# An attention layer without transposes on TensorE: the row of shifts goes transposed through memory, results are scaled untransposed, and the last two heads get seven score banks

## The reference, cut to what matters

```python
x = L0_attn_hidden_states                                   # (4, 2048, 256)
xn = layernorm(x)
# attention
qkv = (xn @ W_qkv).reshape(B, S, 3, 16, 16)                  # q, k, v of (4, 16, 2048, 16)
scores = einsum('bhqd,bhkd->bhqk', q, k) + compute_bias(rel_emb, S, S)
attn = softmax(scores, axis=-1)
out = einsum('bhqk,bhkd->bhqd', attn, v)
out = transpose(out, (0, 2, 1, 3)).reshape(B, S, 256) @ W_out
# feed-forward: two layers with gelu, scaled by the sum of the combine weights of the router
x = x + out + ffn(xn)
```

## Time and profile before

| | |
|---|---|
| median of 3 runs | 3451.89 us (3449.85 to 3497.42) |
| the profiled execution, its own time | 3448.83 us |
| its span in the trace | 3447.1 us |
| PE busy | 3245.1 us (94%) |
| DVE busy | 2769.0 us (80%) |
| ACT busy | 2476.0 us (72%) |
| POOL busy | 1203.8 us (35%) |
| first stage | to about 587 us |
| attention | from 587 to 3376 us, first score matmul at 631 us |
| projection | 3376.7 to 3447 us |

### The profile page before, as it was taken

The page is one execution under the profiler, slowest core; times in us unless marked ns, Lnnn a source line. Parts: engine busy times, 40 slices in busy tenths (PEclk is TensorE's granted clock), DMA queues, the critical chain, the costliest instruction groups (busy, mean ns, idle before and its releaser), DMA issues. The chain is left out here.

```text
span 3447.1 us, 56397 instructions
## 1 busy us (share of the span) xinstructions
PE 3245.1 (94%) x20426; PEld 1573.3 (46%) x20426; DVE 2769.0 (80%) x3046; ACT 2476.0 (72%) x4875; POOL 1203.8 (35%) x1644
## 2 busy tenths in 40 slices
PE   8899997699999999999999999999999999999998
PEld 7788886233333333333333333333333333333337
DVE  5477764588888888888888888888888888888815
ACT  4343443588878887888878888788878887888875
POOL 1112121233433344434444344333443334333430
PEclk9999999799999999999999999999999999999999
DMA  7332323100000000000000000000000000000006
GB/s 183 115 88 74 102 82 101 47 28 28 28 28 28 28 28 28 28 28 28 28 28 28 28 28 28 28 28 28 28 28 28 28 28 28 28 28 28 15 1 199
DMA packets 80480, 156.52 MB, mean 45 GB/s; under 512 B 8088, under 2 KB 48728, under 8 KB 73864
## 3 DMA queue, kind: packets, MB, share of 16 engines
q1 hardware_dynamic: 80200, 152.90, 15.5%
HBM read 101.92 MB, written 56.16 MB: 46 GB/s over the span
## 5 line engine op out<-in xcount | busy, mean ns | idle before, releaser
L905 DVE TENSOR_REDUCE max_half<-ps 128x1 f32<-128x1024 f32 x1984 | 2337.2, 1220 | 337.0 <-PE ps L946 333.6
L832 ACT ACTIVATE prob<-ps 128x512 f32<-128x512 f32 x4096 | 2114.8, 603 | 506.9 <-PE ps L962 506.8
L962 PE MATMUL ps<-q_st,k_st 49*128 49x512 f32 x4096 | 1511.3, 446 | 160.7 <-ACT prob L832 52.5
L946 PE MATMUL ps<-k_st,q_st 48*128 48x512 f32 x3968 | 1569.4, 468 | 0.2 <-DVE max_half L905 0.2
L876 POOL TENSOR_TENSOR prob<-prob,near 128x224 f32<-128x224 f32 (+2 forms) x1408 | 965.1, 691 | 1667.8 <-ACT prob L832 1649.0
L962 PEld LDWEIGHTS ps<-q_st,k_st 49*128 49x128 f32 x4096 | 679.2, 184 | 1334.7 <-ACT prob L832 1142.2
L971 PE MATMUL ps<-prob,vx 128*32 128x512 f32 x4096 | 947.8, 606 | 0.0
L971 PE MATMUL ps<-prob,vr 128*32 128x512 f32 x4096 | 946.1, 604 | 0.0
L946 PEld LDWEIGHTS ps<-k_st,q_st 48*128 48x128 f32 x3968 | 656.3, 184 | 58.7 <-DVE max_half L905 2.5
L608 PE MATMUL ps<-xnt,w_parts 128*128 128x512 f32 x1152 | 276.7, 400 | 16.7 <-DMA k_early<-qk_parts 10.5
L608 PEld LDWEIGHTS ps<-xnt,w_parts 128*128 128x128 f32 x1152 | 218.1, 191 | 70.1 <-DMA k_early<-qk_parts 10.7
(11 more groups left out here) (70 smaller groups left out, 1060.4 us busy)
## 6 DMA issues: line engine op xcount, KB each, us to landing
qk_parts<-parts SPq DMA_DIRECT2D x64, 512.0 KB, 4.6
near<-bias_near SPq DMA_DIRECT2D x64, 352.0 KB, 13.4
q_st<-qk_parts SPq DMA_DIRECT2D x64, 256.0 KB
k_st<-qk_parts SPq DMA_DIRECT2D x64, 256.0 KB
x_sb<-in_L_attn_hidden_states SPq DMA_DIRECT2D x18, 512.0 KB, 6.1
base_rows<-x_sb SPq DMA_DIRECT2D x16, 512.0 KB, 2.9
q_st<-qk_parts SPq DMA_DIRECT2D x64, 128.0 KB
k_st<-qk_parts SPq DMA_DIRECT2D x64, 128.0 KB
```

Of the source, the lines that this page charges most:

```text
L832: nc.scalar.activation(prob[:, kb % PROBS, CH * c:CH * (c + 1)], ps[:, tile_at(kb, c) % RING], ACT.Exp).then_inc(drained, 1)
L905: nc.vector.reduce_max(max_half[:, par % 2, i, half:half + 1], ps[:, MAX_BANK + 2 * half:MAX_BANK + 2 + 2 * half].rearrange("p a n -> p (a ...
L946: mm = nc.tensor.matmul(ps[:, MAX_BANK + c], q_st[u][0:ROWS, P * i:P * (i + 1)], k_st[u][0:ROWS, CH * c:CH * (c + 1)], start=True, stop=True)
L962: nc.tensor.matmul(ps[:, tile_at(kb, c) % RING], k_st[u][:, P * kb:P * (kb + 1)], q_st[u][:, CH * c:CH * (c + 1)], start=True, stop=True). ...
```

## The change

Both kinds of turn go.

- The row of shifts: `max_neg` goes from SBUF to memory (`shift_all`) with a DMA whose memory side is transposed: 2048 pieces of one element. SP waits until it has landed (`shift_stored`), and then loads the row into the stack with a second DMA. It does so right behind the loads at a head's start, for head n + 1.
- The results: ScalarE copies bank 7 to `o_sb` as before (two buffers now). Four DMAs spread the four rows of sums over 128 partitions (`total_sb`, function `totals`), VectorE takes reciprocals after block 6 (`TOTAL_AT`), SP stores them to memory (`recip_all`), waits, and reads them back with four DMAs, each row copied to 16 partitions (`recip_rows`, function `spread`). GpSimd multiplies `o_sb` by it after block 10 (`NORM_AT`), 128x512, and four DMAs put the result in place for the projection (function `keep`).
- The projection has no barrier ahead of it, no packing and no transposes. ScalarE makes the high part, GpSimd (not VectorE) the low part, from SBUF. `W_out` and the first four chunks of `base_rows` are loaded during head 1.
- The last two heads, which have no maxima to make for others, use seven banks for scores (`bank_of`).
- `prob` has three blocks and not four (`PROBS`).

```diff
-PROBS = 4
+PROBS = 3
 LAG = 2
+TURNED = 3
...
+    shift_d = nc.dram_tensor("shift_all", [NH, S], F32).ap()
+    recip_d = nc.dram_tensor("recip_all", [NH, S], F32).ap()
...
+            TOTAL_AT, NORM_AT = 6, 10
+            ALONE = tile_at(NH - LEAD, 0, 0)
+            def bank_of(at):
+                return at % RING if at < ALONE else (at - ALONE) % SUM_BANK
...
             @block.sync
-                def shift(n, u):
-                    wait(sp, drained, 1 if isinstance(n, int) and n == 0 else drained_at(n - 1, SHIFT_AT))
-                    sp.dma_start(q_st[u][ROWS:ROWS + 1, :].bitcast(F32).rearrange("a (i p) -> a i p", p=P),
-                                 shift_row[:, n % 2 if isinstance(n, int) else u % 2, :].bitcast(F32)) \
-                        .then_inc(shift_in[u], 16)
+                def shift(n):
+                    wait(sp, neg_done, n + 1)
+                    sp.dma_start(shift_d[n].rearrange("(i p) -> p i", p=P), max_neg[:, n % 2].bitcast(F32), allow_slow_non_contiguous=True) \
+                        .then_inc(shift_stored, 16)
+                    sp.wait_ge(shift_stored, 16 * (n + 1))
+                    sp.dma_start(q_st[n % GROUP][ROWS:ROWS + 1, :].bitcast(F32), shift_d[n:n + 1]).then_inc(shift_in[n % GROUP], 16)
+                def totals(n):
+                    sp.wait_ge(o_copied, n + 1)
+                    wait(sp, recip_done, n)
+                    for c in range(CPB):
+                        sp.dma_start(total_sb[32 * c:32 * (c + 1)], o_sb[32 * c + D:32 * c + D + 1, n % 2].rearrange("a (g i) -> a g i", i=PIECE)) \
+                            .then_inc(total_in, 16)
+                def spread(n):
+                    sp.wait_ge(recip_done, n + 1)
+                    sp.dma_start(recip_d[n].rearrange("(p i) -> p i", i=PIECE), recip[:]).then_inc(recip_stored, 16)
+                    sp.wait_ge(recip_stored, 16 * (n + 1))
+                    wait(sp, o_done, n)
+                    for c in range(CPB):
+                        sp.dma_start(recip_rows[32 * c:32 * c + D], recip_d[n:n + 1, CH * c:CH * (c + 1)].to_broadcast([D, CH])).then_inc(recip_in, 16)
+                def keep(n):
+                    sp.wait_ge(o_done, n + 1)
+                    for c in range(CPB):
+                        sp.dma_start(attn[b][D * (h % (P // D)):D * (h % (P // D) + 1), h // (P // D), CH * c:CH * (c + 1)],
+                                     o_sb[32 * c:32 * c + D, n % 2]).then_inc(attn_in[b], 16)
...
+                for n in range(NH):
+                    if n + GROUP - 1 < NH:
+                        load(n + GROUP - 1)
+                    if n + 1 < NH:
+                        shift(n + 1)
+                    if n > 0:
+                        totals(n - 1)
+                        spread(n - 1)
+                        keep(n - 1)
...
             @block.gpsimd
+                def normalise(n):
+                    pool.wait_ge(recip_in, 16 * CPB * (n + 1))
+                    nc.gpsimd.tensor_tensor(o_sb[:, n % 2], o_sb[:, n % 2], recip_rows[:], ALU.mult).then_inc(o_done, 1)
...
             @block.vector
+                def reciprocals(n):
+                    dve.wait_ge(total_in, 16 * CPB * (n + 1))
+                    wait(dve, recip_stored, 16 * n)
+                    nc.vector.reciprocal(recip[:], total_sb[:]).then_inc(recip_done, 1)
+                for n in range(NH):
+                    for kb in range(KB):
+                        if n + LEAD < NH:
+                            maxima(n + LEAD, kb)
+                        if kb == TOTAL_AT and n > 0:
+                            reciprocals(n - 1)
...
             @block.tensor
-                def turn_shift(m, par):
-                    wait(pe, neg_done, m + 1)
-                    nc.tensor.transpose(ps[0:KB, SHIFT_AT % RING, 0:P], max_neg[:, par % 2], ident[:]).then_inc(shift_turned, 1)
-                def turn_result(n):
-                    wait(pe, o_copied, n + 1)
-                    for i in range(TPC):
-                        last = nc.tensor.transpose(ps[:, RESULT_AT % RING, P * i:P * (i + 1)], o_sb[:, P * i:P * (i + 1)], ident[:])
-                    last.then_inc(o_turned, 1)
```

More of the change, by code:

```diff
@@ L779, in group @@
-                def group(g, last=False):
-                    for u in range(GROUP):
-                        n = GROUP * g + u
-                        if not (last and u > 0):
-                            load(n + GROUP - 1, (u + GROUP - 1) % GROUP)
-                        if not (last and u == GROUP - 1):
-                            shift(n + 1, (u + 1) % GROUP)
-                load(0, 0)
+                    sp.dma_start(near[u][:], near_d[n % H:n % H + 1].rearrange("a p s c -> (a p) s c")).then_inc(near_in[u], 16)
@@ L1072, in batch @@
+                totals(NH - 1)
+                spread(NH - 1)
+                keep(NH - 1)
+                for b in range(B):
                     for c in range(CPB):
-                        wait(sp, res_done, TPC * (CPB * b + c + 1))
-                        sp.dma_start(out[bass.ds(S * b + CH * c, CH), :].rearrange("(t p) e -> p t e", p=P), base_in[:, c]) \
+                        sp.wait_ge(res_done, TPC * (CPB * b + c + 1))
+                        sp.dma_start(out[S * b + CH * c:S * b + CH * (c + 1), :].rearrange("(t p) e -> p t e", p=P), base_in[:, c]) \
@@ L1075, in batch @@
                             .then_inc(stored[c], 16)
[L1076 to L1086 removed]
+                        if b + (c > 0) in range(1, B):
+                            load_base(b + (c > 0), (c + CPB - 1) % CPB)
@@ L1178, in _ @@
-                turn(0, 0)
-                turn(1, 1)
-                pe.wait_ge(wo_low, 1)
-                batch(0)
-                for b in range(1, B - 1):
-                    batch(b)
-                batch(B - 1)
+                            for x, y in PASSES:
+                                last = nc.tensor.matmul(ps[:, PROJ_BANK + t, 0:E], turned[:, i % TURNED, x, k, P * t:P * (t + 1)], wo_parts[:, y, k],
+                                                        start=k == 0 and (x, y) == PASSES[0], stop=k == KE - 1 and (x, y) == PASSES[-1])
```

527 lines of the change are left out of this document (207 added, 320 removed).

## The result

The changed kernel takes 3901.7 us (median of 4 runs, 3883.89 to 3909.42) beside 3450.9 us before (3447.99 to 3497.42). The ratio is 1.126, 95% interval 1.116 to 1.137: slower by 451 us. The profiled execution took 3907.11 us, its span is 3905.2. In some executions of a kernel TensorE's granted clock is lower for a stretch and the time is some 20 to 47 us longer, as in the 3497.42 us here; the medians hardly feel it.

A forecast was written before the change was run, and what follows sets the result against it. Bound: a loop of latencies through ScalarE, with VectorE 0.25 us to spare a block. 3447.1 - 53 - 18 - 5 + 7 = 3378 without stalls; + 252 + 150 = 3780, so a median of 3785 us, range 3420 to 4200.

The forecast's parts named there:

- The likeliest case: Stall before the reciprocal in heads 1 to 60: X from 2.6 to 9 us, about 3500 to 4030, likeliest 3785; chance 0.62.
- The store's landing: Transposed store of max_neg on SP's queue: lands some 18 us after issue, 13 of queue and 5 of its own.
- The 4.9: Predicted time in us for the transposed store's single elements: 128 on each engine at 38 ns.
- The stall: Sums reach VectorE's reciprocal late and hold TensorE: X - 0.7 us, 4.2 us a head, 60 x 4.2 = 252 us.
- The clock: TensorE's granted clock falls behind each stall: 2.5 us each, 60 x 2.5 = 150 us; nothing if the clock holds.
- The start of the attention: SP waits for the first transposed store before loading heads 1 and 2: 7 us more.
- The turns: Result's turn 0.64 us and shift's turn 0.2 go: 0.85 us a head, 53 us for 62 heads.
- The last two heads: Seven score banks make ScalarE the bound: 17 us, and 1.5 of turns, less about 0.7 at the switch; 18 us gained.
- The projection: From TensorE's last product to the end: 69 us after the change for 73.8 before, 5 us less.
- Both rivals of a fitting chain: The chain fits, no stall: 3383 us, chance 0.10. Gain and stall cancel, stalls under 2 us: 3383 to 3497, chance 0.12.
- X: Time the transposed store's single elements take behind the loads on SP's queue; unknown, taken as 4.9 us.
- The rival of dear elements: X from 9 to 14.7 us: stalls of 8.3 to 14 us and the clock, 4030 to 4370 us; chance 0.16.

The follow-up runs named there:

- the straight store: The changed kernel with max_neg stored untransposed, 128 runs of 64 bytes for 2048 elements, so the row of shifts is permuted: 3377.0 us, ratio 0.978.
- the first experiment: The changed kernel with SP's transposed store, its wait and the row's load put ahead of the five loads of a head: 4144.6 us, ratio 1.200.
- the experiment: The kernel with the loads last on SP's queue (3388.2 us), with three score banks instead of seven in the last two heads: 3402.0 us, ratio 0.990.

## Why the prediction was right

Predicted were 3785 us, with 3420 to 4200 as the range; measured are 3902. The likeliest case, a stall ahead of the reciprocal in each head and a lower clock behind it, is what happened. Step by step:

- **The store's landing.** "Some 18 us after its issue: 13 of queue and 5 of its own". It took 18.4, and the straight store 13.1. The sum is right, and that is in part luck. The 4.9 came from a load at the program's start, and I added it behind `near`, whose landing I left at 13.4. In fact `near` came in only after 17.8 us, delayed by the elements behind it, and the store about 1 us after that: the elements' price sits in the queue and not behind it. Nor is 4.9 what they cost alone, which is 11.4 us; most of that is hidden beside the loads. A reader who had used my 4.9 for empty queues would have been wrong by a factor of two, as I was in the first experiment.
- **The stall**, 4.2 us for TensorE: 4.8 measured, 288 us and not 252 (4.6 as the mean of all 60 heads). The reciprocal's own wait is 6.0 us. The difference between the two, 1.2 us, is what VectorE and the banks had in hand.
- **The clock**, 2.5 us a stall: about 3.9, 232 us and not 150. This is the largest miss, 82 of the 117 us. I had taken a value between the row behind 2.82 us of idle time (1.4 us of loss) and the row behind 42.8 us (4.5), by the length of the idle time. The scale was wrong: in this loop an idle time of 2.8 us costs 3.3 us and not 1.4, and one of 4.6 already as much as one of 8.5 (3.9). The heads spend 11.7 us at the lower level on average, near the 11.2 of the attention's start, the only one of the two rows with the same loop behind it, and far from the 3.4 of the other.
- **The start of the attention**, 7 us: 13 to 15 measured (first score matmul 646.31 for 631.11, the stage itself beginning about 2 us later). SP's first store was issued at 595.06 and done at 611.87, 16.8 us and not 6.7: an element costs more than I took it for, and the store stands behind the loads of head 0, issued from 589.70 on.
- **The turns**, 0.85 us a head: a head without stalls takes 41.9 us for 42.8, 0.9 measured.
- **The last two heads**, 18 us: 13.9 for the banks by the experiment, and the turns' 1.5 on top, which were not measured by themselves. ScalarE runs without gaps there, as predicted.
- **The projection**, 5 us: from the last product to the end it takes 64.3 us (3840.9 to 3905.2) for 73.8 before, 9.5 us less. My sum had 69 us.

The sum with these terms: 3447 - 53 - 18 - 9.5 + 15 + 288 + 232 = 3902, where the span is 3905. It comes so close because the clock's 232 is what was left of the measured head; the 53 and 18 in it are still the forecast's, with 15.4 for the 18 it is 3904.

Both rivals of a fitting chain decide at an X of 0.7 and 2.6 us. The straight store is the first of them made real, at 3377 us where I gave 3383, so its price was right and only its condition failed. The second took stalls under 2 us to be harmless to the clock. That premise fails: in the run with the loads over all engines they were 1.5 us, the clock fell in 40 of 60 heads, and it cost 2.3 us a head. The rival of dear elements (X over 9) has the store alone on its side, 11.4 us in empty queues, and its stall against it: what counts in the kernel is how much the elements add behind the loads, 5.3 us.

## What to carry to other kernels

In these runs a DMA of a few KB was late by the queue it stood in and the number of its pieces, not by its bytes: price it in the place where it is issued, with what stands ahead of it and what is issued next behind it, and put the transfers that are wanted first ahead of the bulk, the whole chain of them: with the first alone ahead the kernel was 6% slower still. Ask in which engine's queue the first wait for it stands and what is queued behind that: moving the one waiting instruction by four blocks, or five DMAs behind others, turned 13% slower into 2% faster. If TensorE stands still for some microseconds in each turn of a loop, charge the stall and the slow work behind it; here the second cost nearly as much as the first, and with short stalls more.

## What the runs showed of the hardware that I had not expected

- A store of 2048 single elements of four bytes from 128 partitions takes 11.4 to 11.7 us in empty queues, where one of the same 8 KB in 128 pieces takes 1.4. Its packets are all recorded in the first 2.5 us, and the DMA share over the whole time is 0.09; what the other nine are spent on isn't shown. Behind two loaded engines the straight store costs nothing that shows beyond the queue, and the transposed one 5.3 us, of which 4.3 are a later landing of the 352 KB that were issued before it. How the elements hold up the loads isn't shown.
- DMAs of 2 KB, which land in 1.8 us in empty queues, took up to 12.7 us behind the loads, though half of them took no more than 3.0.
- TensorE's clock fell to its lower level behind mean stalls of 8.5, 4.6, 2.8 and 1.5 us in this loop and stayed there for 15.3, 11.7, 8.9 and 5.7 us a head, though TensorE was busy all through them (13.59 of the 13.7 us in the head shown). 21 matmuls of 49 rows in a row during the stall did not keep it up in 51 of 60 heads, 20 matmuls of 128 rows did in 50 of 57.
